# GpSimd forms part of the first decay exponents, and the dt sums move inside in-projection chunks

## The reference, cut to what matters

```python
proj = hidden_states @ in_proj_w.T                       # 512 -> 8192 gate, 10240 conv, 128 dt
gate, xBC, dt = jnp.split(proj, [INTER, INTER + CONV_DIM], axis=-1)
xBC = silu(causal_depthwise_conv4(xBC) + conv_b)          # 4 taps
x, Bm, Cm = jnp.split(xBC, [INTER, INTER + NG * SS], axis=-1)
dt = jnp.clip(jax.nn.softplus(dt + dt_bias), 0.001, 100.0)
cs = jnp.cumsum(dt * A, axis=-1)                          # A = -(1..128); chunks of 128 positions
seg = cs[..., :, None] - cs[..., None, :]
Lmat = jnp.where(tri, jnp.exp(seg), 0.0)                  # the decays
scores = jnp.einsum('bclhn,bcshn->bchls', Cc, Bc) * Lmat
Ydiag = jnp.einsum('bchls,bcshp->bclhp', scores, x * dt)
```

## Time and profile before

| | |
|---|---|
| median of 3 runs | 2133.59 us (2131.73 to 2133.9) |
| profiled execution, its own time | 2129.18 us |
| its span | 2127.4 us |
| PE busy | 2087.6 us, 98% of the span |
| DVE, ACT, POOL busy | 1641.0, 1432.5, 1053.0 us (77%, 67%, 49%) |
| DMA | 202.53 MB, mean 95 GB/s |

### The profile page before, as it was taken

The page is one execution under the profiler, slowest core; times in us unless marked ns, Lnnn a source line. Parts: engine busy times, 40 slices in busy tenths (PEclk is TensorE's granted clock), DMA queues, the critical chain, the costliest instruction groups (busy, mean ns, idle before and its releaser), DMA issues.

```text
span 2127.4 us, 34908 instructions
## 1 busy us (share of the span) xinstructions
PE 2087.6 (98%) x12642; PEld 1736.3 (82%) x12652; DVE 1641.0 (77%) x2661; ACT 1432.5 (67%) x3090; POOL 1053.0 (49%) x758
## 2 busy tenths in 40 slices
PE   8999999999999999999999999999999999999999
PEld 7866698887788888888888888888888888888887
DVE  7777773325889898898898989889889898998222
ACT  5498743335978777778777877767877787784332
POOL 5577545451355356354455535634445553555452
PEclk9999999999999999999999999999999999999999
DMA  3000013332343233233223323323322432331332
GB/s 139 1 1 2 1 61 94 95 90 77 131 139 134 72 113 125 74 129 139 90 90 139 134 76 109 127 75 126 139 90 90 139 134 75 110 114 58 96 95 84
DMA packets 65337, 202.53 MB, mean 95 GB/s; under 512 B 7056, under 2 KB 9104, under 8 KB 56976
## 3 DMA queue, kind: packets, MB, share of 16 engines
q1 hardware_dynamic: 65168, 200.31, 27.8%
HBM read 197.39 MB, written 2.88 MB: 94 GB/s over the span
## 4 chain that ended last, share of the span: by engine, by line
PE 91%; DVE 4%; ACT 3%; issue 1%; POOL 0%; DMA 0%; DVEq 0%; SPq 0%; ACTq 0%; POOLq 0%
PE ps L1808 86%; PE ps L2206 3%; PE ps L1993 2%; PE ps L1823 1%; ACT eb L960 0%; DVE bst L1186 0%; DVE x L1590 0%; ACT xTh L688 0%; DVE xTl L1209 0%; ACT pr_a L827 0%; DVE eb L1560 0%; DVE PT L1416 0%; DVE rs L1361 0%; ACT pr_b L827 0%; DMA cst<-cst_in 0%
## 5 line engine op out<-in xcount | busy, mean ns | idle before, releaser
L579 POOL TENSOR_TENSOR wAl<-rawA,wAh 128x512 fp32r<-128x512 f32 x233 | 341.6, 1481 | 364.4 <-ACT wAh L721 363.9
L1808 PE MATMUL ps<-xTh,wAh 128*128 128x512 f32 (+1 forms) x1528 | 419.4, 396 | 4.7 <-DVE xTl L1209 4.7
L1808 PE MATMUL ps<-xTl,wAh 128*128 128x512 f32 (+1 forms) x1528 | 405.9, 387 | 0.0
L1808 PE MATMUL ps<-xTh,wAl 128*128 128x512 f32 (+1 forms) x1528 | 405.2, 387 | 0.0
L1514 DVE SCALAR_TENSOR_TENSOR work<-ps,chp,work 128x510 f32<-128x510 f32 (+2 forms) x465 | 343.2, 743 | 22.7 <-ACT work L923 12.7
L1808 PEld LDWEIGHTS ps<-xTl,wAh 128*128 128x128 f32 x1528 | 285.5, 188 | 60.2
L1808 PEld LDWEIGHTS ps<-xTh,wAl 128*128 128x128 f32 x1528 | 285.2, 188 | 58.4
L1808 PEld LDWEIGHTS ps<-xTh,wAh 128*128 128x128 f32 x1528 | 277.3, 188 | 67.6 <-issue 12.8
L585 POOL TENSOR_TENSOR wBl<-rawB,wBh 128x512 fp32r<-128x512 f32 x108 | 139.8, 1308 | 388.7 <-ACT wBh L725 388.7
L960 ACT ACTIVATE eb<-eb,gc 128x128 f32<-128x128 f32 x1008 | 307.6, 392 | 0.0
L923 ACT ACTIVATE work<-ps,gpar 128x512 f32<-128x512 f32 x155 | 119.4, 771 | 128.8 <-PE ps L1808 96.9
(11 more groups left out here) (210 smaller groups left out, 3960.4 us busy)
## 6 DMA issues: line engine op xcount, KB each, us to landing
eb<-scr_decays SPq DMA_DIRECT2D x62, 1536.0 KB, 6.4
rawA<-ma_in SPq DMA_DIRECT2D x144, 256.0 KB, 6.8
rawA<-fa_in SPq DMA_DIRECT2D x88, 256.0 KB, 2.6
rawB<-mb_in SPq DMA_DIRECT2D x64, 256.0 KB, 2.8
rawB<-fb_in SPq DMA_DIRECT2D x44, 256.0 KB, 2.6
x<-x_in SPq DMA_DIRECT2D x8, 256.0 KB, 6.7
x_out<-x SPq DMA_DIRECT2D x8, 256.0 KB, 2.4
wqraw<-wqkv_in SPq DMA_DIRECT2D x1, 1536.0 KB, 11.1
```

The costliest lines, as they stand in the source:

```text
L579: nc.gpsimd.tensor_tensor(wAl[:, slot, :], rawA[:, slot, :], wAh[:, slot, :].bitcast(F32), ALU.subtract).then_inc(A_lo, 1)
L1808: return nc.tensor.matmul(o, l, r, start=start, stop=end, **kw)
```

## The change

GpSimd gets a function that forms exponents of the first two pairs (with the sign turned, so that the exponential needs no factor), ACT loses them, and the order of the opening changes on ACT, DVE and PE. Lines that declare the new semaphore m_neg_first are left out below, as are signatures.

```diff
@@ GpSimd
+        def first_spans(v, p):
+            if v == 0:
+                pool.wait_ge(m_first[p], 48)
+            else:
+                pool.wait_ge(m_rows[1], 16)
+            pool.wait_ge(m_ctok, p + 1)
+            for h in (0,) if p else range(2):
+                for t in range(4 * p, 4 * p + 4):
+                    e = eb[:, v, h, t, :]
+                    last = nc.gpsimd.tensor_scalar(e, e, ctok[:, t, 2 * v + h:2 * v + h + 1], 0.0, ALU.subtract, ALU.min)
+            last.then_inc(m_neg_first, 1)
...
+        first_spans(0, 0)
+        first_spans(0, 1)
         lo_A(A0G + 5)
+        first_spans(1, 0)
...
@@ ACT: spans, decay_exp, step
-            for h in range(2):
+            for h in (1,) if k == 0 else range(2):
...
+            if k == 0 and p == 1:
+                act.wait_ge(m_neg_first, 2)
+                nc.scalar.activation(e[:, 0, :], e[:, 0, :], ACT.Exp)
+                act.wait_ge(m_neg, 1)
+                nc.scalar.activation(e[:, 1, :], e[:, 1, :], ACT.Exp, scale=-1.0).then_inc(m_exp, 1)
+            elif k < 2 and p == 0:
+                act.wait_ge(m_neg_first, 2 * k + 1)
+                nc.scalar.activation(e, e, ACT.Exp).then_inc(m_exp, 1)
...
+            opening = first and v == 0
             conv_start(gn, conv[0], slot)
-            spans(*vn, 0)
+            if not opening:
+                spans(*vn, 0)
...
@@ ACT: the opening
         layer_hi(4, 5, 5)
+        layer_hi(4, 6, 4)
+        conv_start(0, 2, 1)
+        layer_hi(4, 7, 5)
         dt_act(0, 2)
-        conv_start(0, 2, 1)
-        layer_hi(4, 6, 4)
-        layer_hi(4, 7, 5)
         dt_act(0, 3)
+        dt_act(1, 0)
+        dt_act(1, 1)
         conv_start(0, 4, 1)
+        dt_tokens(0)
+        dt_act(1, 2)
+        dt_act(1, 3)
+        running_sums(0)
+        conv_start(0, 1, 1)
         hi_B(B0G)
         hi_B(B0G + 1)
-        dt_tokens(0)
-        dt_act(1, 0)
-        dt_act(1, 1)
-        dt_act(1, 2)
-        running_sums(0)
-        dt_act(1, 3)
-        conv_start(0, 1, 1)
         conv_start(0, 3, 1)
+        token_sums(0)
         dt_tokens(1)
-        token_sums(0)
         conv_silu(0, 0)
+        running_sums(1)
         conv_silu(0, 2)
         conv_start(0, 5, 1)
-        running_sums(1)
...
-        spans(0, 0, 0)
         end_decays()
         first_exp(0)
+        hi_A(A0G + 5)
         spans(0, 0, 1)
         first_exp(1)
-        hi_A(A0G + 5)
@@ DVE: the opening
         dt_clip(0)
-        taps(0, 2)
+        taps(0, 2, (1,))
         decay_rate(0)
-        taps(0, 4)
+        taps(0, 2, (2, 3))
+        taps(0, 4, (1, 2))
         dt_clip(1)
-        taps(0, 1)
+        taps(0, 4, (3,))
+        taps(0, 1, (1, 2))
         decay_rate(1)
+        taps(0, 1, (3,))
@@ PE: the opening (a product calls between[n] ahead of its matmul n)
-        chunk(0, 6)
-        layer_transpose(4, 6, 4, False)
-        layer_transpose(4, 7, 5, False)
+        chunk(0, 6, {2: lambda: layer_transpose(4, 6, 4, False), 8: lambda: layer_transpose(4, 7, 5, False)})
...
         dt_product(1)
+        chunk(0, 1)
         dt_transpose(0)
-        chunk(0, 1)
-        sums(0)
-        chunk(0, 3)
+        chunk(0, 3, {8: lambda: sums(0)})
         sums_transpose(0)
         pe.wait_ge(m_dts, 5)
         dt_transpose(1)
-        chunk(0, 5)
-        sums(1)
+        chunk(0, 5, {10: lambda: sums(1)})
         chunk(0, 7)
```

More of the change, by code:

```diff
@@ L267, in build @@
     m_neg = sem("m_decay_exponent")
+    m_neg_first = sem("m_first_decay_exponent")
     m_rstd = sem("m_rstd")
@@ L954, in spans @@
                 act.wait_ge(m_first[p], 48)
+                act.wait_ge(m_ctok, p + 1)
             else:
                 act.wait_ge(m_rows[v % 2], 16 * (k // 2 + v % 2))
-            for h in range(2):
+            for h in (1,) if k == 0 else range(2):
                 for t in range(4 * p, 4 * p + 4):
@@ L964, in decay_exp @@
         def decay_exp(v, g, p):
-            act.wait_ge(m_neg, 2 * (g * TPG + v) + p + 1)
+            k = g * TPG + v
             e = eb[:, v % 2, :, 4 * p:4 * p + 4, :].rearrange("p h t q -> p h (t q)")
-            nc.scalar.activation(e, e, ACT.Exp, scale=-1.0).then_inc(m_exp, 1)
+            if k == 0 and p == 1:
[6 more added lines that the diff above has]
+                nc.scalar.activation(e, e, ACT.Exp).then_inc(m_exp, 1)
+            else:
+                act.wait_ge(m_neg, max(2, 2 * k + p - 1))
+                nc.scalar.activation(e, e, ACT.Exp, scale=-1.0).then_inc(m_exp, 1)
         def y_hi(g, v, p):
@@ L1035, in step @@
             gate_silu(gn, gate[1])
-            if first and v == 0:
+            if opening:
                 second_exp()
@@ L1102, in first_exp @@
         def first_exp(p):
+            act.wait_ge(m_first[p], 48)
             e = eb[:, 0, :, NT + 2 * p:NT + 2 * p + 2, :].rearrange("p h t q -> p h (t q)")
@@ L1808, in mm, with product @@
             return nc.tensor.matmul(o, l, r, start=start, stop=end, **kw)
-        def product(o, lh, ll, rh, rl, start=True, end=True, **kw):
+        def product(o, lh, ll, rh, rl, start=True, end=True, between={}, **kw):
             passes = [(a, b) for l, r in ((lh, rh), (lh, rl), (ll, rh)) for a, b in zip(l, r)]
             for n, (a, b) in enumerate(passes):
+                if n in between:
+                    between[n]()
                 last = mm(o, a, b, start and n == 0, end and n == len(passes) - 1, **kw)
@@ L2150, in swiglu, with in_chunk @@
                     last.then_inc(m_out, 1)
-        def in_chunk(g, c):
+        def in_chunk(g, c, between={}):
             tile, half = c // 2, c % 2
@@ L2180, in in_chunk, with chunk @@
             return product(ps[:, chunk_bank(g, c), :], wh, wl, [xTh[:, kc, cols] for kc in range(KC)],
-                           [xTl[:, kc, cols] for kc in range(KC)])
-        def chunk(g, c):
-            in_chunk(g, c).then_inc(m_in, 1)
+                           [xTl[:, kc, cols] for kc in range(KC)], between=between)
+        def chunk(g, c, between={}):
+            in_chunk(g, c, between).then_inc(m_in, 1)
         def bc(g, b):
```

## The result

The changed kernel takes 2137.16 us (median of 13 runs, 2135.7 to 2141.38), the kernel before 2134.31 in the same number (2131.73 to 2138.58). The ratio is 1.0016, 95% interval 1.0008 to 1.0023: 3.4 us slower by the ratio (the medians differ by 2.85), inside 0.2%. The forecast was 0.3 us faster; its range, to 2137.5, just holds the time, but the sign is wrong. From here on TensorE is the tensor engine (PE), VectorE the vector engine (DVE), ScalarE the scalar engine (ACT).

What follows compares the result with a forecast made beforehand. The opening was bounded by late decays behind ScalarE's unbroken chain; tensor-engine idling and slow clock were about 8.6 us. Pair 1's y-products at -1.8 and the clock at +1.5 gave -0.3 us, 2133.3; range 2128.5 to 2137.5.

Steps and rivals of the forecast that it cites:

- The end of the normalised tiles: Last transposes and xTl before the first product of the opening: product starts at 509.8 instead of 510.86, gain 1.1 us.
- The stall before chunk(0, 3): Tensor engine idles 3.1 us waiting for chunk 2's taps; the chunk ends 2.0 us behind the old order.
- The scalar chain: ScalarE from running_sums(0) to pair 0's last exponential: last gate half at 533.7, chain ends at 540.4 against 540.83.
- Most of the work taken away only pays for the stall: Conclusion on ScalarE's opening chain: despite the spans removed, it ends at 540.4 against 540.83.
- GpSimd's price: GpSimd's new 128x128 instructions: 0.5 us each, hidden for the first half and for the second pair.
- The slower rival: GpSimd slower than ACT's need, deciding from 0.7 us per instruction; at 1.1 us the time is 2138.6; chance 0.13.
- The clock: After the 3.1 us stall the granted clock falls, about 1.5 us lost in chunk(0, 3); holding had chance 0.30.
- the 8.6 us that I gave as the most an opening could gain: Tensor engine's idling plus 1.5 us for the clock in the opening, about 8.6 us; no reordering gains more.
- the main case: Stall before chunk(0, 3) with the clock falling: 2133.3, bounds 2131.8 to 2134.5; chance 0.43.
- The sum: Whole kernel: -1.8 us for pair 1's earlier y-products and +1.5 for the clock, -0.3 us, 2133.3.
- the signs that I had listed for being wrong or right: Right: 0.50 clock around 519 to 523, no exponential waiting for GpSimd; wrong: GpSimd above 0.8 us, change after 570.

Runs made afterwards that it cites:

- e3: Changed kernel with the old order of the opening on ScalarE, VectorE and TensorE, GpSimd still forming the spans; 2132.64 us, 0.9994 to the kernel before.
- e1: Changed kernel with the write and reads of the second half's rows issued ahead of two weight loads; 2135.94 us, 1.0010 to the kernel before.
- e8: Kernel before, with three weight loads behind the first rows held until the opening's first silu is done; 2138.18 us, 1.0009 to the kernel before.
- e9: Changed kernel in its new order, with pair 0's second half wholly on ScalarE again; 2140.91 us, 1.0020 to the kernel before.
- e5: e3 with pair 0's second half wholly on ScalarE, GpSimd forming only the two first halves; 2132.82 us, 0.9979 to the kernel before.
- e10: The same kernel as e5 once more, on another set of runs; 2135.44 us, 0.9994 to the kernel before.
- e2: Kernel before with only the new order on ScalarE, VectorE and TensorE, GpSimd doing nothing new; 2137.12 us, 1.0027 to the kernel before.
- e4: Changed kernel with all three taps of chunk 2 ahead of decay_rate(0) on VectorE; 2135.29 us, 1.0003 to the kernel before.
- e6: Kernel before with only the second pair's first half on GpSimd, pair 0 staying with ScalarE; 2134.68 us, 0.9994 to the kernel before.
- e7: Changed kernel with the changes of e1 and e4 together; 2137.28 us, 1.0007 to the kernel before.

## Why the prediction was wrong

**The end of the normalised tiles: right.** 0.58 us of idling where 1.67 were; from the opening's start the product is 1.05 earlier (13.47 against 14.52), 1.1 was said.

**The stall before chunk(0, 3): right.** 3.1 us said, 2.94 measured, with the releaser named.

**The scalar chain: right until it met the rows.** csf(0) was said to be 3.9 late and is 3.9 late (25.55 against 21.66 from the start). The last gate half of ScalarE was to end at 533.7; it ends at 534.29, which is 533.97 on the old time base (0.32 less), 0.3 off. (The prediction's own terms give 533.5.)

**The step that failed: "Most of the work taken away only pays for the stall."** I let the chain run on to 540.4 as if its inputs were there. I had worked out when the *first* half's rows land, and never when the *second* half's do. Their write and three weight loads are issued by the same queue in the order of the code, and the step that I had just computed, csf(0) 3.9 later and csf(1) by much less, is what closes the gap between them. In e3, with the old distance, GpSimd starts on the rows 7.9 us after the write's issue (527.50 to 535.39); the same here would have been 536.9, before ScalarE wants them. They came at 540.9, and ScalarE waited 2.68 us for them, a wait that the forecast does not have at all. That transfers close ahead delay the write is shown by e1 (2.46 us without two of the loads) and by e8 (4.0 us with loads held back in the kernel before).

**GpSimd's price: too low, and read at the wrong place.** I took 0.5 us, it is 0.69 to 0.70 alone (5.56 / 8) and 0.84 beside VectorE (6.69 / 8). I judged by the first half, which was just in time (GpSimd done at 536.33, ScalarE's exponential at 536.66). The four of the second half have no such cover: 2.78 us against ScalarE's 1.28, and a wait of 1.07, which the forecast did not have (and which only takes the place of the four spans that ScalarE was spared, as e9 shows). The eight of pair 1 run later than forecast, until 551.65, then lo_A until 554.6, beside the gates and yTl of pair 0. VectorE before and after:

```profile
552.63 1.84 DVE L1582 SCALAR_TENSOR_TENSOR yTl<-gt,chp,yTh 128x512 fp32r<-128x512 f32 x2 [0.59 <-ACT yTh L974]
```

```profile
545.01 0.85 DVE L1583 TENSOR_TENSOR eb<-eb,cbO 128x512 f32<-128x512 f32 x1 [4.27 <-issue]
545.79 1.21 DVE L1590 TENSOR_TENSOR eb<-eb,cbD 128x1024 f32<-128x1024 f32 x1
...
555.08 2.97 DVE L1612 SCALAR_TENSOR_TENSOR yTl<-gt,chp,yTh 128x512 fp32r<-128x512 f32 x2
```

That is 1.1 us more in the pair of yTl alone, but it is not what times pair 1: e5, e9 and e10 have yTl in 2.2 us instead of 2.97 and a longer B (14.1 against 13.75). ScalarE times it, and its first decay exponential of pair 1 starts, before and after, at

```profile
556.45 1.99 ACT L967 ACTIVATE eb<-eb 128x1024 f32<-128x1024 f32 x2
```

```profile
558.67 1.04 ACT L992 ACTIVATE eb<-eb 128x1024 f32<-128x1024 f32 x1
```

With the last exponential of pair 0 ending at 540.83 and 544.92, B is 1.9 us shorter: the eight spans did pay. Of GpSimd's work beside VectorE ScalarE feels only two waits for gates in B, 0.28 and 0.49. The slower rival had the right engine with the wrong half and price: from 0.7 per instruction on, it said, GpSimd decides; at 0.69 the first half was hidden, as its row shows.

**The clock: wrong in this execution, and not forecastable from the pause.** I expected a fall after 3.1 us. After the same 2.94 us it held in the changed kernel, e1 and e2 and fell in e9. In the changed kernel it held after 3.81 too; in e4 it fell at 3.66, in the kernel before at 2.23 and in e6 at 2.22, in e8 it held after 2.50. Nor does a fall always cost the opening anything. In the kernel before TensorE ran at 0.50 from 544.7 to 548.1 and then waited for the decays all the same (1.12 at 560.08); e8, the same order with the clock at 1.00 there, has the same B (15.61 against 15.62) and waits 1.90. So of the 8.6 us that I gave as the most an opening could gain, the clock's 1.5 was no part of the path to pair 1. It costs where a chain starts at the slow matmuls (e9) or has to wait for them (e4). The upper bound of the main case does not follow either: -1.8 and +2.1 give 2133.9, not 2134.5.

**The sum.** Said: -1.8, and +1.5 for the clock. Measured in the opening: +1.9 with the clock at 1.00 throughout. The difference of 3.7 is on ScalarE. Its spans start at 540.58 on the old time base, where my chain, 540.4 less the 2.7 us from there to its end, has 537.7: 2.9 late for the rows. Its last exponential ends at 544.60 instead of 540.4, 4.2 late, with the wait of 1.07 for GpSimd. From there to the end of pair 1's exponential it took 14.8 us where I had 15.3 (540.4 to 555.7), which gives 0.5 back. Against the kernel before, A is 3.8 longer and B 1.9 shorter. The rest of the 3.4 us is not settled: it is within the spread of the part after the opening, and the wait of 2.41 at 768 may be part of it. Four of the signs that I had listed for being wrong or right went against me: no window at 0.50 around 519, a GpSimd instruction above 0.8 us, an exponential waiting for GpSimd, and more idling after 570.

## What to carry to other kernels

When a step of an in-order opening is moved, list the transfers that its queue issues between this step and the next one of its kind: moving the first of two write-and-read-back pairs later by 4 us and the second by 2 pushes everything between them into the second's way. An engine that is slower per instruction (0.69 against 0.31 us here) helps where its input is early; the half whose input lands last did 1.2 us better on the fast engine when GpSimd would have worked beside VectorE (e5 against e3), and 0.1 better when not (e9 against the changed kernel). No median shows it in the time of the whole kernel. Find the engine whose chain ends last and add up its stretches alone: idle time and a slow clock on another engine, TensorE here, can be free. And split a change that both reorders and offloads before timing it: here one part cost 3 us and the other gained 2, and the sum hid both.

## What was not expected of the hardware

- The granted clock fell after an idle stretch of 2.94 us in one of four kernels with that same stretch, and not after 3.81 in another; it fell after 2.22 (e6) and held after 2.50 (e8). In these traces it can't be read off the length of the last pause alone.
- A write of 256 KB to HBM lands 2.0 to 2.3 us after its issue, and 4.0 to 5.8 us with three loads of 256 KB issued within the last 3 us; with one of them, 2.5 (e1, e7). With the same distances it took 4.9 (e4, e9), 5.2 (e2) and 5.8.
- A GpSimd tensor_scalar with a per-partition operand, subtract and min, on 128x128 float32 takes 0.69 us alone and up to 1.0 beside VectorE (4.02 / 4 in e1). The 128x512 one with one operation took 1.50, so it is far from a quarter of it. VectorE's tensor_scalar of 128x512 with two per-partition operands took 0.54 in the kernel before (at 506.85). The Trainium skill, "GPSIMD Engine Reference" (section "Engine selection"), calls one-input operations roughly line-rate. The trace does not agree: at 128x512 GpSimd needs 2.8 times VectorE's time.
- Two executions of one kernel differ by 3.4 us in the part after the opening, with the same instructions. TensorE waits 0.6 us for a decay product at some group starts and not at others; between 575 and 1900 there are 3 such waits in one execution of e5 and 7 in the other.
